# A graph network of four layers on one core: the last node work of two stages moved beside the first units of the next stage, and the tables of the window sums made in two halves

## The chip, the core and the metric

The kernel runs on one core of one Trainium2 chip, as one program. The metric is the device time of one execution in microseconds (us): the median of 3 runs is 2177.65 us, and they lie between 2176.7 and 2178.26. One further execution was profiled; every row below comes from it.

## What is computed

Input are 4096 nodes with 128 features (`x`) and one dense 4096x4096 float32 matrix `adj`, mostly zero. Four layers follow one another, each on a layer norm and ReLU of `x`, each added to `x`:

```
h = relu(layernorm(x)); x = x + L0(h)       # dinv * (adj + I) * dinv @ (h W0^T + b0)
h = relu(layernorm(x)); x = x + L1(h)       # the same with a batch norm of h W1^T + b1 over the nodes
h = relu(layernorm(x)); x = x + L2(h)       # attention:
    xw = h @ W2; el = xw @ a_l; er = xw @ a_r
    attn = where(adj != 0, exp(leaky_relu(el[:, None] + er[None, :])), 0)
    out = (attn / attn.sum(-1)) @ xw + b
h = relu(layernorm(x)); x = x + L3(h)       # three heads and two GRU cells:
    hp = (adj' > 0) @ hW;  hm = (adj' < 0) @ hW          # adj' is adj without its diagonal
    e_plus, e_minus = leaky_relu([hp hm] @ a), leaky_relu([hm hp] @ a)
    att = softmax over the neighbours of e_plus or e_minus, by the sign of adj'
    edge_support = mean over heads of (att * adj') @ hW
    L3 = diag(adj) * gru(adj' @ h, h) + diag(adj) * gru(edge_support, h)
```

## The kernel before, in words

The adjacency matrix doesn't fit on the chip. It is streamed once by rows (to sum the degrees) and then once for each of four passes in **units**: a unit is 128 x 2048 float32 (1 MB), that is, four blocks of 128 source nodes by 512 target nodes. A **chunk** (`c`, 0 to 7) is 512 target nodes and takes 8 units (`g`, 0 to 7), so a pass has 64 units, numbered `n = 8c + g`. The sums of a chunk gather in one or two PSUM banks, and after the chunk its **node work** follows: PSUM to SBUF, turn, scale, add to `x`, norm (statistics on VectorE in `norm_in`, square root on ScalarE in `root`, `norm_out` on VectorE), turn on TensorE (`turn_h`), ReLU on ScalarE, and the next layer's projection (`project` on TensorE, `project_keep` on ScalarE, `agg_project` or `gat_project` on VectorE).

The stages in order of time:

- **deg** sums the rows and makes the first projection.
- **agg0, agg1** are the first two layers. For a unit, ScalarE rounds it to `a_hi` (L502), VectorE takes the rest `a_lo` (L853), and TensorE runs 12 matmuls of 512 columns (L1364 to L1366).
- **gat** is the attention layer. For a unit, VectorE makes half the scores (`gat_max`, L928), ScalarE the other half (L548) and the exponentials (L551, L555), VectorE multiplies with the mask of the unit, in place (L948, the **product**), and TensorE runs 16 matmuls of 129 columns (L1394), each of two passes, so 32 in the profile. The scores of a unit stand in `gunit(n)`, one of three buffers. They need the projection of their targets' chunk (`reg4`) and, for each block of sources, a column of `el02`, `er02`, `er08`, made by ScalarE from `elr` (L518 to L520).
- **edge**, the score pass, sums both score tables `sp_all` and `sm_all` over the positive and the negative neighbours, and `h` over `adj'`. For a unit, VectorE makes two fp8 masks (`masks`, L976 and L977), which are also stored to DRAM, and TensorE runs 8 short matmuls (L1421) and 4 float32 matmuls of 512 columns (L1426, of two passes each, so 8 in the profile). Four pairs of masks fit in `made`.
- **norm**, the sums pass (L1500), reads the stored masks back (`load_masks`, L365) and sums exponentials in windows, so that the softmax can be normalised. Its tables `vp` and `vm` are made by VectorE and ScalarE from the scores of all nodes (L1078 to L1092, "prep"), one after the other: add a shift (3 instructions), cap, exponential on ScalarE (L598, L601), choose, and split into three bf16 parts. The masks come into eight buffers, `kept`. Buffers 4 to 7 lie over the temporaries of the edge GRU cell, so their loads wait for `s_ct["edge"]` to reach 8, the turn of the last chunk's cell (`turn_cells("edge", C)`).
- **out** makes the weights again, multiplies (L1538) and ends with the second GRU cell.

The order of the work is written out by hand: each engine has a program of its own (`@block.tensor` and so on), executes it strictly in that order, and waits on semaphores. `s_ln[p]` counts the norm steps of pass `p`, `s_hturn` the turns of `h`, `s_proj` the projections, `s_pkeep` and `s_pkeep_act` the projections kept, `s_mm[p]` the units multiplied, `s_gy` the products, `s_gexp` the exponentials, `s_mask` the mask pairs, `s_prep` the steps of prep. SyncE issues the unit loads in order into a ring of 8 slots (6 in edge), each when its slot's last unit has been multiplied.

At the end of a stage the node work of its last chunks has nothing beside it. At the handover from agg1 to gat the TensorE program is:

```
                project(p, C - 1)
                turn_sum(p, C)
                turn_h(p, C)
                project(p, C)
            pe.wait_ge(s_pkeep_act, C)
```

and only then come the units of gat. From gat to edge it is `turn_h("gat", C - 1)`, `project`, `turn_h("gat", C)`, `project`, and a wait for all of `s_pkeep["gat"]`. VectorE and ScalarE have the matching ends. From edge to norm TensorE waits for `s_prep` to reach its last step.

Of the kernel before, what the change touches and what calls it, by code (L numbers as in the profile page):

```python
# [39 lines left out]
AHEAD = 2  # L40
GBUFS = 3
# [10 lines left out]
PREP_HEAD, PREP_SIGN = 9, 8  # L52
# [37 lines left out]
def build(nc, x_d, rows_d, cols_d, diag_d, w_d, gru_d, col_d, row_d, masks_d, lines_d, out_d):  # L90
    with ExitStack() as ctx:
# [335 lines left out]
        def _(act):  # L427
# [39 lines left out]

            for p in ("agg0", "agg1"):
# [16 lines left out]
                for c in range(C):  # L485
                    for g in range(G):
# [29 lines left out]
            act.wait_ge(s_pkeep["agg1"], C)  # L516
            elr_v = elr[:, :].rearrange("p (t h) -> p h t", h=2)
            act.activation(el02[:, :], elr_v[:, 0, :], ACT.Exp, scale=SLOPE).then_inc(s_e02, 1)  # L518
            act.activation(er02[:, :], elr_v[:, 1, :], ACT.Copy, scale=SLOPE).then_inc(s_e02, 1)
            act.activation(er08[:, :], elr_v[:, 1, :], ACT.Copy, scale=1 - SLOPE).then_inc(s_e02, 1)  # L520
            act.wait_ge(s_pkeep_act, C)
            act.wait_ge(s_e02, 3)
            act.wait_ge(s_mm["agg1"], G * C)
# [11 lines left out]
            for c in range(C):  # L535
                for g in range(G):
# [149 lines left out]
        def _(dve):  # L686
# [137 lines left out]
            for p in ("agg0", "agg1"):  # L824
# [11 lines left out]
                for c in range(C):  # L836
                    s = Steps(dve, s_ln[p], LN_STEPS[p], c - 1)
                    for g in range(G):
# [17 lines left out]
                agg_project(p, C - 1)  # L856
                s = Steps(dve, s_ln[p], LN_STEPS[p], C - 1)
                agg_nodes_in(p, C, s)
# [741 lines left out]
```

## Time and profile before

| what | us |
|---|---|
| median of 3 runs | 2177.65 |
| profiled execution, its time | 2176.56 |
| profiled execution, span from first to last instruction | 2174.6 |
| TensorE matmuls busy | 1916.5 (88%) |
| VectorE busy | 1650.9 (76%) |
| ScalarE busy | 1245.5 (57%) |
| stage gat, first matmul to last | 653.1 to 928.0 |
| stage edge, first matmul to last unit's end | 945.0 to 1258.5 |
| stage norm, first matmul to last | 1288.2 to 1411.5 |

In the page and the answers, PE is TensorE's matmuls, PEld its weight loads, DVE is VectorE, ACT ScalarE, SP SyncE. A timeline row has start and duration in us, engine, line, operation, output and inputs, shapes, the count of instructions merged, and in brackets the engine's idle time before and what released it. An instruction group's duration runs from its first start to its last end. A row of stretches has the busy time of each engine, then the granted TensorE clock as a share of 2.4 GHz (so 0.50 is 1.2 GHz), the share of DMA and GB/s.

### The profile page before, as it was taken

What the parts mean: (1) busy time and instruction counts of PE and PEld (TensorE: products, weight loads), DVE (VectorE), ACT (ScalarE), POOL (GpSimd) and SP (SyncE); (2) the same over time, 40 slices, a digit from 0 to 9 for tenths busy, and PEclk for the clock granted to TensorE, in tenths of its full rate; (3) what the DMA queues carried; (4) which work ended last, traced back from release to release, by engine and by line L of the source; (5) the groups of instructions that cost most, each with busy time, mean ns of one, the idle gap of its engine ahead of it and who ended that gap; (6) DMA issues with size and microseconds to landing.
All of it is one profiled execution on the core that took longest, in us unless ns stands there. A gap on an engine that the chain in (4) does not pass through costs nothing.

```text
span 2174.6 us, 21337 instructions
## 1 busy us (share of the span) xinstructions
PE 1916.5 (88%) x7805; PEld 1166.7 (54%) x7805; DVE 1650.9 (76%) x2422; ACT 1245.5 (57%) x1386; POOL 0.8 (0%) x7
## 2 busy tenths in 40 slices
PE   2336999699979889879999959999999999999997
PEld 1224888478859888834444426644444444444443
DVE  4668998698849989855655743398898898888985
ACT  3445666366649898800000010198888788887873
POOL 0000000000000000000000000000000000000000
PEclk9999999899989999989999979999999999999998
DMA  9998999488857766659899749732333323233220
GB/s 389 429 429 349 344 338 345 166 306 319 321 194 252 247 222 249 232 181 334 298 321 324 272 162 326 248 99 109 107 122 106 111 102 126 95 118 126 91 83 10
DMA packets 81559, 489.46 MB, mean 225 GB/s; under 512 B 8449, under 2 KB 12546, under 8 KB 36402
## 3 DMA queue, kind: packets, MB, share of 16 engines
q1 hardware_dynamic: 77138, 485.94, 60.9%
q10 hardware_dynamic: 4320, 2.20, 0.3%
q8 instruction: 60, 0.98, 0.2%
q14 instruction: 41, 0.34, 0.1%
HBM read 452.36 MB, written 35.75 MB: 224 GB/s over the span
## 4 chain that ended last, share of the span: by engine, by line
PE 52%; DVE 11%; ACT 6%; issue 1%; DMA 0%; DVEq 0%
PE bank L1538 25%; PE bank L1426 11%; PE bank L1500 5%; PE bank L1394 4%; DVE work L1208 3%; ACT work L555 2%; ACT work L548 2%; PE bank L1421 2%; ACT work L551 1%; DVE reg L1208 1%; PE bank L1449 1%; PE bank L1450 1%; DVE ring L948 1%; PE bank L1520 1%; DVE work L1186 1%
## 5 line engine op out<-in xcount | busy, mean ns | idle before, releaser
L1538 PE MATMUL bank<-work,reg 128*128 128x512 f32 x960 | 423.1, 596 | 17.3 <-DVE ring L1157 11.4
L1208 DVE TENSOR_TENSOR work<-work,ring 128x1536 f32<-128x1536 f32 x160 | 280.5, 1753 | 67.7 <-ACT work L677 66.8
L853 DVE TENSOR_TENSOR a_lo<-ring,a_hi 128x2048 fp32r<-128x2048 f32 x128 | 290.8, 2288 | 31.4 <-ACT a_hi L502 30.5
L1538 PEld LDWEIGHTS bank<-work,reg 128*128 128x128 f32 x960 | 181.9, 191 | 246.7 <-issue 220.3
L502 ACT ACTIVATE a_hi<-ring 128x2048 fp32r<-128x2048 f32 x128 | 244.2, 1913 | 78.5 <-PE bank L1366 78.5
L1394 PE MATMUL bank<-reg,ring 128*128 128x129 f32 x2048 | 243.8, 281 | 34.3 <-DVE ring L948 34.3
L1394 PEld LDWEIGHTS bank<-reg,ring 128*128 128x128 f32 x2048 | 238.2, 197 | 39.2 <-DVE ring L948 29.3
L1538 PE MATMUL bank<-reg 128*128 128x512 f32 x576 | 252.4, 592 | 0.0
L677 ACT ACTIVATE work<-work 128x1536 f32<-128x1536 f32 x160 | 235.3, 1471 | 26.2 <-DVE work L1186 26.2
L1426 PE MATMUL bank<-ring,reg 128*128 128x512 f32 x512 | 237.8, 607 | 0.0
L1364 PE MATMUL bank<-a_hi,s_hi 128*128 128x512 f32 x512 | 207.4, 405 | 20.5 <-DVE a_lo L853 20.5
L1366 PE MATMUL bank<-a_hi,s_lo 128*128 128x512 f32 x512 | 201.9, 394 | 0.0
L1365 PE MATMUL bank<-a_lo,s_hi 128*128 128x512 f32 x512 | 200.7, 392 | 0.0
L1538 PEld LDWEIGHTS bank<-reg 128*128 128x128 f32 x576 | 109.4, 190 | 137.8 <-issue 134.4
L1208 DVE TENSOR_TENSOR reg<-reg,ring 128x1536 f32<-128x1536 f32 x96 | 167.9, 1751 | 0.0
L948 DVE SCALAR_TENSOR_TENSOR ring<-ring,work 128x2048 f32<-128x2048 f32 x64 | 146.6, 2291 | 17.7 <-ACT work L555 17.5
L1426 PEld LDWEIGHTS bank<-ring,reg 128*128 128x128 f32 x512 | 92.4, 190 | 120.0 <-issue 120.0
L653 ACT ACTIVATE work<-reg,ne 128x512 f32<-128x512 f32 x224 | 152.4, 708 | 0.0
L677 ACT ACTIVATE reg<-reg 128x1536 f32<-128x1536 f32 x96 | 141.4, 1472 | 13.6 <-DVE reg L1186 13.6
L1500 PE MATMUL bank<-ring,reg 128*126 128x512 fp8e4 x512 | 115.5, 384 | 20.3 <-DVE reg L1092 16.7
L1364 PEld LDWEIGHTS bank<-a_hi,s_hi 128*128 128x128 f32 x512 | 97.4, 190 | 42.5 <-issue 24.2
L445 ACT ACTIVATE work<-ring 128x2048 f32<-128x2048 f32 x32 | 61.1, 1910 | 101.6 <-DMA ring<-in_adj_rows 101.6
(215 smaller groups left out, 2158.1 us busy)
## 6 DMA issues: line engine op xcount, KB each, us to landing
ring<-in_adj_units SPq DMA_DIRECT2D x320, 1024.0 KB, 4.9
ring<-in_adj_rows SPq DMA_DIRECT2D x32, 2048.0 KB, 17.0
masks<-work SPq DMA_DIRECT2D x64, 512.0 KB, 8.9
ring<-masks SPq DMA_DIRECT2D x64, 512.0 KB, 4.6
reg<-lines SPq DMA_DIRECT2D x8, 768.0 KB, 10.2
ring<-lines SPq DMA_DIRECT2D x8, 768.0 KB, 7.9
out<-ring ACTq DMA_DIRECT2D x8, 256.0 KB, 2.3
gru<-in_cells SPq DMA_DIRECT2D x1, 768.0 KB
```

What stands on the lines that cost most here:

```text
L502: act.activation(a_hi[:, (g % 4) * UNIT:(g % 4 + 1) * UNIT], ring[:, ring_at(p, g)], ACT.Copy).then_inc(s_ahi[p], 1)
L677: act.activation(tiles(n), tiles(n), ACT.Exp, scale=-1.0).then_inc(s_exp, 1)
L853: dve.tensor_tensor(a_lo[:, ring_at(p, g)], ring[:, ring_at(p, g)], a_hi[:, (g % 4) * UNIT:(g % 4 + 1) * UNIT].bitcast(F32), ALU.subtract) ...
L948: dve.scalar_tensor_tensor(y, y, 0.0, gunit(n), ALU.not_equal, ALU.mult).then_inc(s_gy, 1)
L1208: dve.tensor_tensor(tv, tv, spread(ring[:, ring_at("out", g, q * W, W)], HEADS, 1), ALU.mult).then_inc(s_y, 1)
L1364: pe.matmul(acc[:, :], sh, hi, start=begin, stop=False)
L1365: pe.matmul(acc[:, :], sh, lo, start=False, stop=False)
L1366: last = pe.matmul(acc[:, :], sl, hi, start=False, stop=end)
L1394: last = pe.matmul(gat_acc(c, i), y[:, q * W + i * P:q * W + (i + 1) * P], xw[:, m, :], start=m == 0 and i % 2 == 0, stop=m == T - 1 and i ...
L1426: last = pe.matmul(nacc[:, :], reg1[:, t * P:(t + 1) * P], ring[:, ring_at("edge", g, q * W, W, c=c)], start=t == 0, stop=t == T - 1)
L1500: last = pe.matmul(bank[c % 2][0:VCOLS, :], table[:, t * VCOLS:(t + 1) * VCOLS], mask[:, q * W:(q + 1) * W], start=t == 0 and table is vp, ...
L1538: last = pe.matmul(bank[1 + k][:, :], h, tiles(c * T + t)[:, k * W:(k + 1) * W], start=t == 0, stop=t == T - 1)
```

## The change

It does four things.

1. **agg1 to gat.** The tail of agg1's last chunk is taken out of its place and put between gat's first units. On TensorE `turn_h("agg1", C)` comes after gat unit 1 and `project("agg1", C)` after unit 2; a unit of chunk 0 waits for the kept projection of its own sources alone. On VectorE `gat_max(0)` comes first, the node work of the last chunk before unit 0's product, `norm_out` before unit 2's and `agg_project` before unit 4's. On ScalarE the four steps come before units 1 to 4. The columns `el02`, `er02`, `er08` are made in two parts: for source blocks 0 to 23 (`EARLY`) during agg1's last chunk, for 24 to 31 before gat unit 5. Three memsets move behind unit 3's product, one into agg1.
2. **gat to edge.** VectorE makes the masks of units 0 and 1 before the node work of gat's last chunk, those of 2 and 3 inside it, and TensorE runs edge units 0 and 1 before `turn_h("gat", C)`, unit 2 before `project("gat", C)`.
3. **prep in two halves.** `vp` and `vm` are made for source blocks 0 to 15, then for 16 to 31, each with its own exponentials. TensorE waits for the first half before norm unit 0 and for the second before unit 4.
4. ScalarE runs the edge cell's gates after the second exponential of four instead of the first of two.

The diff, cut to its core:

```diff
+EARLY = T - 2 * Q
-PREP_HEAD, PREP_SIGN = 9, 8
+PREP_HEAD, PREP_SIGN, PREP_PARTS = 9, 8, 2
...
+            def exponentials(first, end):
+                act.wait_ge(s_pkeep["agg1"], end // Q)
+                v = elr[:, 2 * first:2 * end].rearrange("p (t h) -> p h t", h=2)
+                tiles_ = slice(first, end)
+                act.activation(el02[:, tiles_], v[:, 0, :], ACT.Exp, scale=SLOPE).then_inc(s_e02, 1)
...
+                        if p == "agg1" and c == C - 1 and g == 6:
+                            exponentials(0, EARLY)
...
                 finish_hT(p, C - 1)
-                project_keep(p, C - 2)
                 keep_sum(p, C)
-                root(p, C - 1)
-                finish_hT(p, C)
-                project_keep(p, C - 1)
                 if p == "agg0":
+                    project_keep(p, C - 2)
+                    root(p, C - 1)
+                    finish_hT(p, C)
+                    project_keep(p, C - 1)
...
-            act.wait_ge(s_pkeep_act, C)
-            act.wait_ge(s_e02, 3)
-            act.wait_ge(s_mm["agg1"], G * C)
+            act.wait_ge(s_pkeep_act, EARLY // Q)
...
+                    if c == 0 and g == 1:
+                        project_keep("agg1", C - 2)
+                    if c == 0 and g == 2:
+                        root("agg1", C - 1)
+                    if c == 0 and g == 3:
+                        finish_hT("agg1", C)
+                    if c == 0 and g == 4:
+                        project_keep("agg1", C - 1)
+                    if c == 0 and g == 5:
+                        exponentials(EARLY, T)
+                    if n < 7:
+                        act.wait_ge(s_e02, 3 if g < EARLY // Q else 6)
                     if n >= GBUFS:
                         act.wait_ge(s_gy, n - GBUFS + 1)
+                    else:
+                        act.wait_ge(s_mm["agg1"], G * C - 3 + n)
...
-            act.wait_ge(s_prep, PREP_HEAD + 2)
-            act.activation(vtmp[1], vtmp[1], ACT.Exp).then_inc(s_vexp, 1)
-            gates("edge", C)
-            act.wait_ge(s_prep, PREP_HEAD + PREP_SIGN + 2)
-            act.activation(vtmp[1], vtmp[1], ACT.Exp).then_inc(s_vexp, 1)
+            for i in range(2 * PREP_PARTS):
+                act.wait_ge(s_prep, PREP_HEAD + i * PREP_SIGN + 2)
+                act.activation(vtmp[1][:, 0:VT // PREP_PARTS], vtmp[1][:, 0:VT // PREP_PARTS],
+                               ACT.Exp).then_inc(s_vexp, 1)
+                if i == 1:
+                    gates("edge", C)
             candidate("edge", C)
...
             gat_max(0)
+            agg_project("agg1", C - 1)
             for c in range(C):
...
+                    if n == 0:
+                        sa = Steps(dve, s_ln["agg1"], LN_STEPS["agg1"], C - 1)
+                        agg_nodes_in("agg1", C, sa)
+                    if n == 2:
+                        dve.wait_ge(s_hturn["agg1"], C - 1)
+                        sa.inc(norm_out(sa, "agg1", C - 1, C))
+                        sa.done()
+                    if n == 4:
+                        agg_project("agg1", C)
+                        clear_tables()
                     if n + 1 < C * G:
                         gat_max(n + 1)
...
-            s = Steps(dve, s_ln["gat"], LN_STEPS["gat"], C - 1)
-            gat_nodes_in(C, s)
-            gat_project(C - 1)
-            gat_nodes_out(C, s)
-            gat_project(C)
...
             masks(0)
+            masks(1)
+            s = Steps(dve, s_ln["gat"], LN_STEPS["gat"], C - 1)
+            gat_nodes_in(C, s)
+            masks(2)
+            gat_project(C - 1)
+            gat_nodes_out(C, s)
+            masks(3)
+            gat_project(C)
...
-            for sign, v in ((0, vp), (1, vm)):
+            for part, sign in itertools.product(range(PREP_PARTS), range(2)):
+                v = (vp, vm)[sign]
+                span = slice(part * T // PREP_PARTS, (part + 1) * T // PREP_PARTS)
...
-            pe.wait_ge(s_pkeep_act, C)
...
+                    if c == 0:
+                        pe.wait_ge(s_pkeep_act, g + 1)
                     pe.wait_ge(s_gy, n + 1)
...
                     last.then_inc(s_gmm, 1)
+                    if n == 1:
+                        turn_h("agg1", C)
+                    if n == 2:
+                        project("agg1", C)
...
             project("gat", C - 1)
-            turn_h("gat", C)
-            project("gat", C)
...
-                        pe.wait_ge(s_ln["gat"], C * LN_STEPS["gat"])
+                        pe.wait_ge(s_ln["gat"], (C - 2) * LN_STEPS["gat"] + GAT_TAKEN)
+                if c == 0:
+                    pe.wait_ge(s_pkeep["gat"], (g + 1) * U_STEPS)
                 pe.wait_ge(s_mask, n + 1)
...
-            pe.wait_ge(s_pkeep["gat"], C * U_STEPS)
             for c in range(C):
                 for g in range(G):
                     edge_unit(c * G + g)
+                    if c == 0 and g == 1:
+                        turn_h("gat", C)
+                    if c == 0 and g == 2:
+                        project("gat", C)
...
-            pe.wait_ge(s_prep, PREP_HEAD + 2 * PREP_SIGN)
...
+                    if c == 0 and g % (G // PREP_PARTS) == 0:
+                        pe.wait_ge(s_prep, PREP_HEAD + (g // (G // PREP_PARTS) + 1) * 2 * PREP_SIGN)
                     pe.wait_ge(s_mload[n % MLOADS], 16 * (n // MLOADS + 1))
```

How the rows stand in the programs (line numbers of the changed file are larger; L1241, L1286, L1288, L1291, L1394 of before are L1288, L1333, L1335, L1338, L1445 there).

**TensorE, end of agg1 and start of gat.** `bank<-ident` is a turn, `hT` and `wts` rows are a projection, `reg,ring` rows gat's units (16 matmuls each). Before, then the change:

```order
L1366 MATMUL bank<-a_hi,s_lo 128x512
L1286 MATMUL bank<-hT,wel 128x512
L1288 MATMUL bank<-wlr,hT 128x2 x4
L1291 MATMUL bank<-wts,hT 128x128 x4
L1241 MATMUL bank<-ident,outT 128x128 x4
L1241 MATMUL bank<-ident,hn 128x128 x4
L1286 MATMUL bank<-hT,wel 128x512
L1288 MATMUL bank<-wlr,hT 128x2 x4
L1291 MATMUL bank<-wts,hT 128x128 x4
L1394 MATMUL bank<-reg,ring 128x129 x288
```

```order
L1413 MATMUL bank<-a_hi,s_lo 128x512
L1333 MATMUL bank<-hT,wel 128x512
L1335 MATMUL bank<-wlr,hT 128x2 x4
L1338 MATMUL bank<-wts,hT 128x128 x4
L1288 MATMUL bank<-ident,outT 128x128 x4
L1445 MATMUL bank<-reg,ring 128x129 x32
L1288 MATMUL bank<-ident,hn 128x128 x4
L1445 MATMUL bank<-reg,ring 128x129 x16
L1333 MATMUL bank<-hT,wel 128x512
L1335 MATMUL bank<-wlr,hT 128x2 x4
L1338 MATMUL bank<-wts,hT 128x128 x4
L1445 MATMUL bank<-reg,ring 128x129 x240
```

The last turn of `hn` now stands behind the first two units of gat, the last projection behind the third; before, both stood ahead of all of them.

**ScalarE, end of agg1 and start of gat.** L474 (L485) is the ReLU into `hT`, L464 and L465 are `project_keep`, L483 is `keep_sum`, L430 (L432) `root`, L518 the first of the columns, L548, L551, L555 (L566, L569, L573) are the scores and exponentials of a unit. Before, all of it stands ahead of unit 0; then, from the changed program, units 1 to 3:

```order
L483 ACTIVATE outT<-bank 128x512
L430 ACTIVATE rstd<-rstd 128x4
L474 ACTIVATE hT<-bank 128x512
L464 ACTIVATE reg<-bank 128x4x128
L465 ACTIVATE reg<-bank 128x512
L518 ACT_TABLE_LOAD
L518 ACTIVATE el<-elr 128x32
L519 ACTIVATE er<-elr 128x32
L520 ACTIVATE er<-elr 128x32
L548 ACTIVATE work<-reg,er 128x512 x2
```

```order
L566 ACTIVATE work<-reg,er 128x512 x2
L569 ACTIVATE work<-work 128x1024
L573 ACTIVATE work<-work,er 128x512 x2
L432 ACT_TABLE_LOAD
L432 ACTIVATE rstd<-rstd 128x4
L566 ACTIVATE work<-reg,er 128x512 x2
L569 ACT_TABLE_LOAD
L569 ACTIVATE work<-work 128x1024
L573 ACTIVATE work<-work,er 128x512 x2
L485 ACTIVATE hT<-bank 128x512
L566 ACTIVATE work<-reg,er 128x512 x2
```

The square root of the last norm now stands between units 1 and 2, with a table load before it and one behind it, and the ReLU before unit 3; before, one load (for L518) followed the square root.

**VectorE, end of gat and start of edge.** L879 to L735 (L900 to L754) are the node work of gat's last chunk, L976 and L977 (L1011, L1012) a pair of masks. Before, then the change:

```order
L948 SCALAR_TENSOR_TENSOR ring<-ring,work 128x2048 x2
L879 TENSOR_TENSOR den<-bank,el 128x2 x2
L882 TENSOR_SCALAR den<-den 128x4
L883 RECIPROCAL den<-den 128x4
L884 TENSOR_TENSOR den<-den,el 128x4
L887 SCALAR_TENSOR_TENSOR x<-bank,den,x 128x128 x4
```

```order
L988 SCALAR_TENSOR_TENSOR ring<-ring,work 128x2048 x2
L995 TENSOR_TENSOR ring<-ring,offdiag 128x128 x4
L1011 TENSOR_SCALAR work<-ring 128x2048
L1012 TENSOR_SCALAR work<-ring 128x2048
L1011 TENSOR_SCALAR work<-ring 128x2048
L1012 TENSOR_SCALAR work<-ring 128x2048
L900 TENSOR_TENSOR den<-bank,el 128x2 x2
L903 TENSOR_SCALAR den<-den 128x4
```

Two pairs of masks now stand between the last product and the node work.

## Rows read from the trace of the kernel before

**Rows 1.** The page, part 1: busy time, share of the span, instructions.

```profile
PE 1916.5 (88%) x7805; PEld 1166.7 (54%) x7805; DVE 1650.9 (76%) x2422; ACT 1245.5 (57%) x1386; POOL 0.8 (0%) x7
```

**Rows 2.** Waits of TensorE: us in total, times, longest us.

```profile
PE bank L1394 <- DVE ring L948: 34.3, 24, 9.6
```

**Rows 3.** Timeline, TensorE at the handover from agg1 to gat.

```profile
625.78 0.40 PE L1366 MATMUL bank<-a_hi,s_lo 128*128 128x512 f32 x1
...
627.68 1.14 PE L1291 MATMUL bank<-wts,hT 128*128 128x128 f32 x8
...
653.06 37.20 PE L1394 MATMUL bank<-reg,ring 128*128 128x129 f32 x310 [9.62 <-DVE ring L948]
```

**Rows 4.** Timeline, ScalarE and VectorE there and in gat's chunk 0.

```profile
629.83 0.60 ACT L483 ACTIVATE outT<-bank 128x512 f32<-128x512 f32 x1
...
631.67 1.13 DVE L811 SCALAR_TENSOR_TENSOR x<-bank,dinv,x 128x128 f32<-128x128 f32 x4 [2.65 <-PE bank L1241]
...
634.26 0.17 DVE L735 TENSOR_SCALAR rstd<-mv 128x4 f32<-128x4 f32 x1
...
652.83 1.00 DVE L928 TENSOR_SCALAR work<-reg,elr,er 128x512 f32<-128x512 f32 x2
...
654.02 2.29 DVE L948 SCALAR_TENSOR_TENSOR ring<-ring,work 128x2048 f32<-128x2048 f32 x1 [0.19 <-ACT work L555]
...
674.40 2.29 DVE L948 SCALAR_TENSOR_TENSOR ring<-ring,work 128x2048 f32<-128x2048 f32 x1 [0.19 <-ACT work L555]
```

**Rows 5.** Timeline, ScalarE at a square root inside gat.

```profile
694.14 1.28 ACT L430 ACT_TABLE_LOAD   x1
```

**Rows 6.** Stretches, TensorE and its granted clock after gat's first matmul.

```profile
656.00:657.00 1.00, 1.00 (x6) 0.50 0.00 0
657.00:658.00 1.00, 1.00 (x7) 0.53 0.00 0
```

**Rows 7.** Timeline, handover from gat to edge.

```profile
920.71 2.29 DVE L948 SCALAR_TENSOR_TENSOR ring<-ring,work 128x2048 f32<-128x2048 f32 x1 [0.16 <-ACT work L555]
...
928.06 0.23 DVE L879 TENSOR_TENSOR den<-bank,el 128x2 f32<-128x2 f32 x2 [5.05 <-PE bank L1394]
...
929.14 1.06 PE L1297 MATMUL bank<-wa,reg 128*128 128x6 f32 x8 [0.69 <-ACT reg L528]
...
934.27 1.11 DVE L742 TENSOR_SCALAR hn<-x,mv,rstd 128x128 f32<-128x128 f32 x4
...
939.87 0.18 DVE L908 COPY work<-bank 128x24 f32<-128x24 f32 x1 [4.49 <-PE bank L1297]
...
941.61 0.89 DVE L960 TENSOR_TENSOR ring<-ring,offdiag 128x128 f32<-128x128 f32 x4
...
944.81 1.22 DVE L976 TENSOR_SCALAR work<-ring 128x2048 fp8e4<-128x2048 f32 x1
...
959.00 0.61 PE L1421 MATMUL bank<-work 128*32 128x512 fp8e4 x8
...
963.18 0.62 PE L1421 MATMUL bank<-work 128*32 128x512 fp8e4 x8
```

**Rows 8.** Timeline, handover from edge to norm.

```profile
1265.31 1.70 DVE L1078 TENSOR_TENSOR work<-e,shift 128x448 f32<-128x448 f32 x3
...
1269.29 1.56 DVE L1086 SCALAR_TENSOR_TENSOR work<-work 128x1344 f32<-128x1344 f32 x1 [1.39 <-ACT work L598]
...
1288.20 0.43 DVE L997 TENSOR_SCALAR ring<-ring 128x512 f32<-128x512 f32 x1
...
1288.22 9.37 PE L1500 MATMUL bank<-ring,reg 128*126 128x512 fp8e4 x32 [16.73 <-DVE reg L1092]
...
1292.34 0.69 DVE L1009 SCALAR_TENSOR_TENSOR ring<-ring 128x512 f32<-128x512 f32 x1
...
1297.42 0.60 PE L1241 MATMUL bank<-ident,ring 128*128 128x128 f32 x4
...
1301.56 8.85 PE L1500 MATMUL bank<-ring,reg 128*126 128x512 fp8e4 x40 [3.54 <-DMA ring<-masks]
```

**Rows 9.** Stretches with all engines, the granted clock between edge and norm.

```profile
1272.00:1280.00 8.00, 0.00 (x0) 0.00 (x0) 7.17 (x8) 1.42 (x3) 0.00 (x0) 0.73 0.45 188
...
1299.00:1301.50 2.50, 0.00 (x0) 0.00 (x0) 0.00 (x0) 0.00 (x0) 0.00 (x0) 1.00 0.98 342
```

More of the change, by code:

```diff
@@ L1 @@
+import itertools
 from contextlib import ExitStack
@@ L837, in _ @@
                     s = Steps(dve, s_ln[p], LN_STEPS[p], c - 1)
+                    if p == "agg1" and c == 1:
+                        dve.memset(xw[:, :, P:P + 1], 1.0)
                     for g in range(G):
@@ L894, in gat_nodes_out @@
             def gat_nodes_out(c, s):
-                dve.wait_ge(s_hkept, c - 1)
+                if c == 1:
+                    dve.wait_ge(s_hturn["agg1"], C)
+                else:
+                    dve.wait_ge(s_hkept, c - 1)
                 s.inc(norm_out(s, "gat", c - 1, c))
@@ L923, in gat_max @@
                 c, g = n // G, n % G
+                if n < 7:
+                    dve.wait_ge(s_e02, 3 if g < EARLY // Q else 6)
+                    dve.wait_ge(s_pkeep_act, EARLY // Q)
                 if n >= GBUFS:
                     dve.wait_ge(s_gy, n - GBUFS + 1)
+                else:
+                    dve.wait_ge(s_mm["agg1"], G * C - 3 + n)
                 for q in (0, 1):
@@ L1072, in _ @@
             s.link(dve.memset(top[:, 16:17], 0.0))
-            for sign, v in ((0, vp), (1, vm)):
+            for part, sign in itertools.product(range(PREP_PARTS), range(2)):
+                v = (vp, vm)[sign]
+                span = slice(part * T // PREP_PARTS, (part + 1) * T // PREP_PARTS)
+                mine = [a[:, 0:VT // PREP_PARTS] for a in vtmp]
+                TP = T // PREP_PARTS
                 e_v = e6[:, :].rearrange("p (t h k) -> p t h k", h=2, k=HEADS)
-                arg, capped, rest = (a.rearrange("p (t v) -> p t v", v=KW) for a in vtmp)
-                parts = [v.rearrange("p (t v) -> p t v", v=VCOLS)[:, :, i * KW:(i + 1) * KW] for i in range(3)]
+                arg, capped, rest = (a.rearrange("p (t v) -> p t v", v=KW) for a in mine)
+                parts = [v.rearrange("p (t v) -> p t v", v=VCOLS)[:, span, i * KW:(i + 1) * KW] for i in range(3)]
                 for k in range(HEADS):
                     last = dve.tensor_tensor(arg[:, :, k * WINDOWS:(k + 1) * WINDOWS],
-                                             e_v[:, :, sign, k:k + 1].to_broadcast([P, T, WINDOWS]),
+                                             e_v[:, span, sign, k:k + 1].to_broadcast([P, TP, WINDOWS]),
                                              shift[:, k * WINDOWS:(k + 1) * WINDOWS].unsqueeze(1)
-                                             .to_broadcast([P, T, WINDOWS]), ALU.add)
+                                             .to_broadcast([P, TP, WINDOWS]), ALU.add)
                 s.link(last)
-                s.inc(dve.tensor_scalar(vtmp[1], vtmp[0], LIFT, None, ALU.min))
-                dve.wait_ge(s_vexp, sign + 1)
-                s.link(dve.scalar_tensor_tensor(vtmp[2], vtmp[0], LIFT, vtmp[1], ALU.is_le, ALU.mult))
+                s.inc(dve.tensor_scalar(mine[1], mine[0], LIFT, None, ALU.min))
+                dve.wait_ge(s_vexp, 2 * part + sign + 1)
+                s.link(dve.scalar_tensor_tensor(mine[2], mine[0], LIFT, mine[1], ALU.is_le, ALU.mult))
                 s.link(dve.tensor_copy(parts[0], rest))
@@ L1384, in _ @@
                     pe.wait_ge(s_ln["gat"], (c - 2) * LN_STEPS["gat"] + GAT_TAKEN)
+                elif c == 1:
+                    pe.wait_ge(s_pkeep_act, C)
+                    pe.wait_ge(s_pkeep["agg1"], C)
                 else:
```

45 lines of the change are left out of this document (22 added, 23 removed).

## The prediction, as it was put on record

> **What bounds the kernel.** I read the page first: TensorE is busy for 88% of the span, VectorE for 76% [rows 1]. So the time is TensorE's, and it can only be won where TensorE stands still or where it follows another engine. The list of waits shows where it follows one: in gat it waits 24 times for VectorE's product, 34.3 us in all, and 9.62 of that is the pause before the first unit [rows 2, 3]. Then I read the timeline at the three handovers that the change touches. From agg1 to gat the last matmul of agg1 ends at 626.2 and gat's first starts at 653.1 [rows 3]; from gat to edge TensorE is free at 930.2 [rows 7] and the first edge matmul comes at 945.0; from edge to norm it waits 16.73 us for the tables and, after four units, 3.54 us more for masks [rows 8]. What an earlier start is worth depends on what paces the stage behind it. In gat's chunk 0 the products come every 3.40 us, (674.40 - 654.02)/6, each 0.19 us after ScalarE's last exponential: ScalarE paces, with VectorE (1.00 + 2.29) close behind [rows 4]. In edge, units stand 4.18 us apart [rows 7], all of it TensorE.
>
> **First handover, agg1 to gat.** I follow the new order with the old durations.
>
> - agg1 ends at 626.2. `keep_sum`, 0.60 [rows 4], no longer waits for the projection of chunk 6 and is done at 626.8. TensorE ends that projection at 628.8 [rows 3] and turns the sum at once, 0.6 as for the turn of the cell [rows 8]: 629.4. The node work, L811 to L735, takes 2.76 [rows 4]: 632.2. Scores 1.0, product 0 2.29: it ends at 635.5. Before, it ended at 652.9 (676.7, the end of product 7 [rows 4], less 7 x 3.40).
> - That is 17.4 us, but ScalarE, the pacing engine, now has the tail's work between its units. Unit 1: the projection kept (2 x 0.60) hides behind VectorE's node work; its exponentials end at 635.6. Unit 2: two table loads of 1.28 [rows 5], 0.2, and 3.5 for the unit: 642.0, product at 644.3.
> - TensorE starts unit 0 at 635.5. A unit is 3.5: ten of them took 37.2 [rows 3], and their first 4.5 us ran at 0.50, 1.2 GHz, until 657.5 [rows 6]. TensorE again comes out of a pause, so unit 0 ends at 641.2 and unit 1 at 644.7. The last turn (0.6) and the ReLU (0.6) follow: ScalarE starts unit 3 at 645.9, and product 3 ends at 651.7. TensorE's unit 2 and the projection (2.8, from 626.0 to 628.8 [rows 3]) end at 651.6, the copies at 652.8, product 4 at 658.6. The second part of the columns adds 0.5: product 5 at 662.5, then 3.4 each, product 7 at 669.3 against 676.7.
> - **7.4 us earlier.** From there VectorE and ScalarE go on as before, so it lasts. Chunk 1's node work needs TensorE's unit 7, done by some 675, and VectorE reaches it at 677.
>
> The row prices a table load at 1.28 us, with the next instruction right behind it. The Trainium skill (ScalarE: Activation LUTs, What ACT_TABLE_LOAD costs) gives about 2.66 us for every switch with the drain, and its rule is to batch by table set, which this edit breaks: by that the two loads would cost 2.8 more, half hidden by TensorE's unit 1, and the gain here would be 5.6. I go by the row. The first part of the columns, with its load, lies in agg1 ahead of ScalarE's last two roundings. TensorE is the engine that ends agg1, so I cost it at nothing; if ScalarE has no lead there, it is 1.28 + 0.6, about 2 us. The memsets (under 1 us) lie in VectorE's wait for ScalarE.
>
> The ends: 0, if TensorE stays at the lower level through units 0 and 1 and the projection (3.5 + 1.3 and 2.8 later); 8.4, if it never falls. I take 7.4, by the clock's return [rows 6].
>
> **Second handover, gat to edge.** The last product ends at 923.0 [rows 7]. Clearing and the first mask pair take 3.2 (941.61 to 944.81), a pair 2.3: 928.5 for two. The node work, the small tables of chunk 6 and the norm took 928.06 to 935.38, 7.3; with pair 2 among them they end at 938.1, pair 3 at 940.4. TensorE is free at 930.2 and runs units 0 and 1 to 938.6 (the clock is up, it has just left gat). `hn` copied (0.6) and turned (0.6): 939.3. Unit 2 to 943.5, projection 1.06 to 944.5, unit 3 to 948.7. VectorE makes the last small tables from 944.5 (939.87 to 941.61, 1.7) and pair 4 by 948.6. With some 0.05 us for each handing over, unit 4 starts at 949.1 against 963.18 [rows 7]: **14 us**, and TensorE paces edge to its end, so all of it lasts. Six units are loaded ahead, and the queue of SyncE has the same order as before, a load behind each store. Ends: 11.7, if one mask pair comes late on this tight path; 14.6, if nothing hands over.
>
> **Third handover, edge to norm.** Now a sign's table takes half of (1288.20 - 1265.31), 11.44 us [rows 8]. An instruction on 1344 elements takes 1.56 and one on 512 0.69: a fixed part of 0.155. Each sign has 11 instructions in its chain (ten of VectorE, one of ScalarE), so half a table takes 5.72 + 11 x 0.155/2 = 6.6. TensorE may start after two, at 1278.5 instead of 1288.2, and runs four units (9.37) to 1287.9. This is 9.7 us earlier, and I expect none of it to last. Unit 4 needs a mask whose buffer is freed by the turn of the edge cell, and the cell stands on VectorE behind all four half tables: 1265.31 + 26.4 = 1291.7, then 4.83 (1288.20 to 1293.03), 1296.5. Before, VectorE had the cell at 1293.0 and TensorE turned it at 1297.4, after its four units. So what was hidden, 4.4 us of slack, is eaten by 3.5 us of added fixed cost: the turn starts 0.9 earlier, takes 0.6 more if the clock is down, the mask load takes its 3.5 as before, and unit 4 starts 0.3 earlier. But TensorE has stood still for 8.6 us before the turn. In the stretch 1272 to 1280, without a matmul, the clock fell [rows 9]; before unit 4, in a pause of 3.5 us behind busy units, it was 1.00 [rows 9]. So unit 4 starts at 1.2 GHz, and some 4.5 us there cost half, 2.3. **Net 2.0 us lost.** Ends: 5 lost, if the 22 added instructions cost twice the fixed part (3.4 later); 4.4 gained, if they are free and the clock stays.
>
> **Sum.** 7.4 + 14.0 - 2.0 = 19.4. The profiled execution takes 2176.6, so 2157.2; the median of the runs shown lies 1.1 above it, at 2177.65, which would give 2158.3. I say 2158. The ends of all three together would be 2170 and 2149.
>
> **The rivals.**
>
> - *The third handover gains.* If the half tables cost no fixed part and the clock holds, the sum is up to 26.8: 2151 to 2155. For it: the 4.4 us of slack. Against it: instructions of 24 elements still take 0.18 [rows 7].
> - *The tail costs ScalarE what it costs.* ScalarE has no spare time in chunk 0. If the loads cost more than the rows say, or the projection runs at 1.2 GHz (2.8 more), the first term is 1 to 3: about 2164. For it: the 0.50 behind a pause [rows 6]. Against it: TensorE works without a pause from 645 to 651.
> - *The second handover doesn't do what it says.* Edge reads 1 MB and writes 0.5 MB in 4.18 us, 376 GB/s, more than the 342 seen beside an idle TensorE [rows 9]. If transfers pace edge once the six loaded units are used, an earlier start is given back there: 2157 + 14, about 2172. Against it: the same pace stood before in the same chunk.
> - *Slower.* TensorE's clock stays at 1.2 GHz through both first chunks, because the tail's pauses are now spread among the first units. Gat units take 7.0: chunk 0 would end at 698 instead of letting node work start at 684.5, 13.8 lost. Eight edge units cost 4.2 more each, 33.4 against 14 won. With the third term, 35 lost: 2212. It decides at 636 to 641: if TensorE isn't at full clock by its unit 2, it is this. Against it: the clock rose 4.5 us after the first unit's start [rows 6].
>
> **How the numbers follow.** Forecast (2154 to 2162) 0.62, third handover gains 0.10, costly tail 0.16, transfers 0.08, slower 0.04. The range of 2152 to 2167 takes in the first, the third and most of the second. About 0.2%, 4.4 us, is what a measurement of this kernel can tell from no change; 2172 is just past it. So faster 0.93, within it 0.03, slower 0.04.
>
> **What would show it.** In the changed profile: product 0 of gat ends near 635.5 and product 7 near 669; TensorE's edge unit 4 starts 21 us earlier than before (7.4 and 14); norm's first matmul comes 31 us earlier, but its unit 4 only some 22; the granted clock is 0.50 at that unit. It is wrong if edge shows waits for masks, if gat's later chunks are longer than before, or if unit 4 of norm moved with unit 0.

## The result, and the profile after

The change takes 2153.26 us (median of 5 runs, 2152.86 to 2155.35) against 2178.26 for the kernel before (5 runs, 2176.7 to 2179.56): a ratio of 0.9888, interval 0.9877 to 0.9899, so 22 to 27 us less. Run again on another occasion (`change_again` below) it gave 0.9894 (0.9878 to 0.9909). The forecast was 2158, within 2152 to 2167. The profiled execution of the change took 2154.86, its span is 2153.1, 21.5 less than before.

The waits of TensorE in the changed kernel (us in total, times, longest):

```profile
PE bank L1445 <- DVE ring L988: 36.8, 26, 6.1
...
PE bank L1288 <- DVE ring L1044: 14.8, 2, 8.6
...
PE bank L1561 <- issue: 8.3, 1, 8.3
...
PE bank L1561 <- DMA ring<-masks: 3.6, 1, 3.6
```

The waits for gat's products are about as long in all as before (36.8 us against 34.3 [rows 2]), in more and shorter pieces. The pause before the first norm unit has gone from 16.73 us [rows 8] to 8.3 (the profile names no releaser for it; it ends 0.1 us behind the second half table), but a new one stands behind it: the turn of the edge cell (L1288) waits 8.6 for the cell (L1044). Then the mask load is waited for as before.

The handover from agg1 to gat, timeline of the changed kernel, TensorE, then VectorE, then ScalarE:

```profile
634.75 9.82 PE L1445 MATMUL bank<-reg,ring 128*128 128x129 f32 x64 [6.09 <-DVE ring L988]
644.41 0.60 PE L1288 MATMUL bank<-ident,hn 128*128 128x128 f32 x4
```

```profile
649.13 2.29 DVE L988 SCALAR_TENSOR_TENSOR ring<-ring,work 128x2048 f32<-128x2048 f32 x1 [4.76 <-ACT work L573]
...
666.33 2.29 DVE L988 SCALAR_TENSOR_TENSOR ring<-ring,work 128x2048 f32<-128x2048 f32 x1 [0.20 <-ACT work L573]
```

```profile
634.74 1.28 ACT L432 ACT_TABLE_LOAD   x1
...
637.48 1.28 ACT L569 ACT_TABLE_LOAD   x1
...
645.04 0.60 ACT L485 ACTIVATE hT<-bank 128x512 f32<-128x512 f32 x1 [3.98 <-PE bank L1288]
```

Unit 0 starts at 634.75 instead of 653.06 [rows 3], but units 0 and 1 take 9.82 us together: the granted clock is 0.50 until 639.8 and 1.00 from there on. ScalarE stands still for 3.98 us until the turn behind them is done, and product 3 waits 4.76 for ScalarE. Product 7 ends at 668.6 instead of 676.7 [rows 4].

The handover from gat to edge, timeline of TensorE:

```profile
921.04 1.06 PE L1344 MATMUL bank<-wa,reg 128*128 128x6 f32 x8 [0.69 <-ACT reg L532]
922.03 0.61 PE L1478 MATMUL bank<-work 128*32 128x512 fp8e4 x8
...
930.69 0.63 PE L1288 MATMUL bank<-ident,reg 128*128 128x128 f32 x4 [0.24 <-ACT reg L537]
...
940.56 0.61 PE L1478 MATMUL bank<-work 128*32 128x512 fp8e4 x8
```

The first edge unit follows the projection of chunk 6 at once, and from there to unit 4 the rows show one wait, 0.24 us. Unit 4 starts at 940.56 against 963.18 [rows 7].

The handover from edge to norm, timeline of VectorE, then TensorE:

```profile
1242.49 1.00 DVE L1125 TENSOR_TENSOR work<-e,shift 128x224 f32<-128x224 f32 x3
...
1269.22 0.43 DVE L1032 TENSOR_SCALAR ring<-ring 128x512 f32<-128x512 f32 x1
```

```profile
1255.92 9.62 PE L1561 MATMUL bank<-ring,reg 128*126 128x512 fp8e4 x32 [8.32 <-issue]
...
1274.12 1.12 PE L1288 MATMUL bank<-ident,ring 128*128 128x128 f32 x4 [8.58 <-DVE ring L1044]
...
1278.81 10.15 PE L1561 MATMUL bank<-ring,reg 128*126 128x512 fp8e4 x40 [3.58 <-DMA ring<-masks]
...
1288.80 0.60 PE L1288 MATMUL bank<-ident,outT 126*128 126x126 f32 x4
```

In the kernel before, that last turn, the first turn of norm's sums, stands here:

```profile
1310.24 0.60 PE L1241 MATMUL bank<-ident,outT 126*128 126x126 f32 x4
```

Norm's first matmul is 32.3 us earlier than before, its unit 4 only 22.75, and the turn behind the five units that start there 21.4: five units that took 8.85 [rows 8] take 10.15. Where the difference of 21.4 us comes from, handover by handover: agg1 itself ended 0.6 earlier in this execution, 7.5 came at the first handover, 14.5 at the second, 0.2 between edge's end and the tables, and 1.4 was lost at the third. The 0.6 is within the spread between executions: agg1 ends between 625.48 and 626.73 in the three profiles whose agg1 is that of the kernel before (`before`, `second_only`, `halves_only`), and between 624.64 and 626.02 in the eleven that have the first part of the columns and a memset in its last chunk.

### The profile page after: what moved, and what is told of

It is laid out like the page before. It is cut to its first block, busy times and chain, and to the rows that moved or that the text cites. A ratio compares the mean times of both kernels' runs of the same rounds, so it can differ in the third digit from the quotient of the medians.

```text
span 2153.1 us, 21391 instructions
## 1 busy us (share of the span) xinstructions
PE 1910.1 (89%) x7805; PEld 1162.6 (54%) x7805; DVE 1652.7 (77%) x2442; ACT 1248.5 (58%) x1393; POOL 0.8 (0%) x7
## 4 chain that ended last, share of the span: by engine, by line
PE 70%; DVE 15%; DMA 7%; ACT 6%; issue 2%; SPq 0%; DVEq 0%; ACTq 0%
PE bank L1599 25%; PE bank L1483 10%; DMA ring<-in_adj_rows 6%; PE bank L1411 5%; PE bank L1413 5%; PE bank L1412 5%; PE bank L1561 5%; PE bank L1445 4%; DVE work L1255 3%; ACT work L573 2%; ACT work L566 2%; DVE a_lo L874 2%; PE bank L1478 2%; DVE reg L1255 1%; PE bank L1288 1%
## 5 line engine op out<-in xcount | busy, mean ns | idle before, releaser
L1599 PE MATMUL bank<-work,reg 128*128 128x512 f32 x960 | 423.0, 596 | 17.3 <-DVE ring L1204 11.4
L1445 PE MATMUL bank<-reg,ring 128*128 128x129 f32 x2048 | 244.9, 281 | 36.9 <-DVE ring L988 36.8
L1445 PEld LDWEIGHTS bank<-reg,ring 128*128 128x128 f32 x2048 | 238.7, 197 | 42.4 <-DVE ring L988 32.5
L696 ACT ACTIVATE work<-work 128x1536 f32<-128x1536 f32 x160 | 235.3, 1471 | 26.1 <-DVE work L1233 26.1
```

Source lines behind the costliest of these rows:

```text
L696: act.activation(tiles(n), tiles(n), ACT.Exp, scale=-1.0).then_inc(s_exp, 1)
L1445: last = pe.matmul(gat_acc(c, i), y[:, q * W + i * P:q * W + (i + 1) * P], xw[:, m, :], start=m == 0 and i % 2 == 0, stop=m == T - 1 and i ...
L1599: last = pe.matmul(bank[1 + k][:, :], h, tiles(c * T + t)[:, k * W:(k + 1) * W], start=t == 0, stop=t == T - 1)
```

## The experiments

Each was run beside the kernel before on one chip, but not all on the same one; the medians of two variants are comparable only through their ratios to the kernel before. Since the medians spread by one or two us, I also measured four stretches in each profile: from agg1's last matmul to the end of gat's product 7, from the end of product 63 to the start of edge unit 4, from the first instruction of the tables to the first turn of norm's sums, and from there to the end. Norm's units 4 to 8, part of the third stretch, have a column of their own.

| kernel | median us (before, same chip) | ratio, interval | agg1 to product 7 | product 63 to edge unit 4 | tables to first turn | of it units 4 to 8 | rest |
|---|---|---|---|---|---|---|---|
| before | - | - | 50.5 | 40.2 | 44.9 | 8.85 | 864.3 |
| the change | 2153.26 (2178.26) | 0.9888, 0.9877 to 0.9899 | 43.0 | 25.7 | 46.3 | 10.15 | 864.3 |
| first_only | 2168.93 (2178.03) | 0.9955, 0.9939 to 0.9972 | 43.5 | 40.5 | 45.1 | 8.85 | 864.4 |
| second_only | 2162.68 (2178.03) | 0.9934, 0.9917 to 0.9951 | 50.1 | 25.7 | 45.1 | 8.85 | 864.4 |
| halves_only | 2178.54 (2178.03) | 1.0003, 0.9993 to 1.0013 | 50.1 | 40.5 | 47.6 | 11.27 | 861.8 |
| no_halves | 2155.35 (2178.03) | 0.9892, 0.9875 to 0.9908 | 43.4 | 25.7 | 45.9 | 10.53 | 864.6 |
| cell_between | 2151.38 (2177.52) | 0.9880, 0.9864 to 0.9897 | 42.8 | 25.7 | 42.0 | 10.66 | 864.5 |
| filler_norm | 2150.32 (2177.52) | 0.9876, 0.9860 to 0.9893 | 42.8 | 25.7 | 44.5 | 8.82 | 861.8 |
| turn_early | 2150.74 (2177.52) | 0.9879, 0.9862 to 0.9895 | 39.1 | 25.7 | 47.9 | 11.69 | 861.8 |
| filler_gat | 2155.29 (2177.52) | 0.9897, 0.9880 to 0.9913 | 41.9 | 25.7 | 47.2 | 11.02 | 864.7 |
| change_again | 2155.17 (2177.69) | 0.9894, 0.9878 to 0.9909 | 43.4 | 25.7 | 48.3 | 11.83 | 861.8 |
| both_mended | 2148.03 (2177.69) | 0.9861, 0.9846 to 0.9876 | 39.1 | 25.7 | 42.0 | 10.69 | 864.6 |
| both_and_filler | 2143.37 (2177.69) | 0.9841, 0.9827 to 0.9854 | 39.8 | 25.7 | 40.2 | 8.85 | 864.2 |
| quarters | 2161.14 (2177.69) | 0.9921, 0.9906 to 0.9936 | 43.1 | 25.7 | 55.3 | 11.40 | 861.8 |

**One part at a time.** `first_only`, `second_only` and `halves_only` hold one handover each; `no_halves` is the change with

```diff
-PREP_HEAD, PREP_SIGN, PREP_PARTS = 9, 8, 2
+PREP_HEAD, PREP_SIGN, PREP_PARTS = 9, 8, 1
```

and the edge cell's gates back behind the first exponential.

> Only the handover from agg1 to gat is changed; the other two stand as in the kernel before. My account (7.4 us won there) expects gat's product 7 to end near 668.6 to 669.3 and the whole to be 7 to 8 us faster than the kernel before, about 2169 to 2170.5. If the tail costs ScalarE what it costs (the costly-tail rival), it is 1 to 3 us. If the measured 25 us of the change contain a gain that is in none of the three handovers, it will show here as more than 9.

> Only the handover from gat to edge is changed. My account expects 14 to 14.5 us less than the kernel before, about 2163 to 2164, with edge unit 4 at some 948.6 instead of 963.2 and every later stage moved by the same. If transfers pace edge, the last edge unit ends less than 5 us earlier and the gain is under 5.

> Only the tables of the sums pass are made in two halves. My account expects a loss of 1 to 2 us against the kernel before (2179 to 2180): norm's first matmul 9 to 10 us earlier, its unit 4 within 0.5 us of before, then the lower clock. The rival (halves gain what TensorE starts earlier) expects 4 to 9 us less, about 2169 to 2174.

> The change with the tables whole again, both other handovers as in the change. My account expects it 1 to 2 us faster than the change, so 23 to 25 us faster than before on the same chip. If the halves won something, it is slower than the change by that much.

The first part alone is worth 9.1 us by the medians (the interval allows 6 to 13) and 7.0 by its stretch. 9.1 is just past the 9 that was to show a gain outside the three handovers, but the profile has none: its other stretches are within 0.4 us of those before, and its span is 6.6 shorter. The second is worth 15.4 by the medians and 14.5 by its stretch. So the costly tail (1 to 3 us) and the transfers as a pace (under 5) are out: in `second_only` edge unit 4 starts 15.7 earlier, of which 1.2 lie ahead of that handover, and the last edge unit is 15.7 earlier too. The halves alone made no difference in the whole (0.5 us more, which the interval doesn't tell from nothing) where 1 to 2 more were expected, but the timeline of TensorE in `halves_only` shows the step:

```profile
1279.59 9.13 PE L1507 MATMUL bank<-ring,reg 128*126 128x512 fp8e4 x32 [7.10 <-issue]
1297.78 1.12 PE L1247 MATMUL bank<-ident,ring 128*128 128x128 f32 x4 [9.07 <-DVE ring L1011]
1302.63 11.27 PE L1507 MATMUL bank<-ring,reg 128*126 128x512 fp8e4 x40 [3.73 <-DMA ring<-masks]
```

The four units start 8.6 us earlier than in the profile of before (9.5 measured from the tables' start, which came 0.8 later in this execution), and unit 4 1.1 later (0.2 from the tables' start), at the lower clock; the stretch is 2.7 longer. That `no_halves` is faster than the change is not shown by the times: it is 22.7 us below the kernel before, where 23 to 25 were expected, the change 25.0 and `change_again` 22.5. By the stretches, four profiles with whole tables (before, `first_only`, `second_only`, `no_halves`) have 44.9 to 45.9 and five with halves and nothing else there (the change, `halves_only`, `turn_early`, `filler_gat`, `change_again`) 46.3 to 48.3: means 45.3 and 47.5. Where it is lost can be read from the rows. Unit 4 starts 35.5 to 36.5 us behind the tables' start in the four and 36.3 to 36.6 in the five, so at that point the halves win and lose almost nothing; the units 4 to 8 behind it take 8.85 in three of the four and 10.53 in `no_halves`, against 10.15 to 11.83 in the five. So the lower clock behind a pause isn't the halves' alone: `no_halves` had it too, with the clock at 0.71 in the first us of unit 4.

Whether this loss lasts to the end of the kernel is not shown. The last stretch of the table is 2.5 us shorter in three of the five (the last section says where), and from the tables' start to the end the four take 909.2 to 910.5 and the five 909.3 to 911.9, which overlap; the means differ by 0.6.

**Who holds norm's unit 4?** `cell_between` moves the cell on VectorE between the halves, and its turn from behind unit 3 to behind unit 1:

```diff
                 s.link(dve.tensor_copy(parts[2], rest))
+                if part == 0 and sign == 1:
+                    sc = Steps(dve, s_gv["edge"], CELL_STEPS, C - 1)
+                    cell_in("edge", C, sc)
+                    cell_end("edge", C, sc)
...
-                    if c == 0 and g == 3:
+                    if c == 0 and g == 1:
                         turn_cells("edge", C)
```

> The change, but VectorE does the last edge cell after the first half of the tables instead of after the second, ScalarE its tanh there, and TensorE turns it after norm unit 1 instead of unit 3, so the masks of units 4 to 7 are fetched early. If the cell's turn and the mask load were what held unit 4, unit 4 now starts when the second half is ready: 1255.9 + 4.9 + 13.4 = 1274.2 instead of 1278.8, 4 to 5 us less than the change, and no wait for masks there. If the cell wasn't the holder, nothing changes.

TensorE in `cell_between`:

```profile
1255.04 5.96 PE L1562 MATMUL bank<-ring,reg 128*126 128x512 fp8e4 x16 [8.51 <-issue]
1260.83 0.60 PE L1289 MATMUL bank<-ident,ring 128*128 128x128 f32 x4
1261.27 3.62 PE L1562 MATMUL bank<-ring,reg 128*126 128x512 fp8e4 x16
1273.09 10.66 PE L1562 MATMUL bank<-ring,reg 128*126 128x512 fp8e4 x40 [8.21 <-DVE reg L1139]
```

The tables began at 1241.60 there and at 1242.49 in the change, so unit 4 starts 31.5 us behind them instead of 36.3: 4.8 earlier, and it waits for the table's last part (L1139), not for masks. The cell and the mask load behind it were the holder. The stretch is 42.0, below the 44.9 to 45.9 of whole tables: with the cell between them, the halves do gain. By the medians it is 26.1 us below the kernel before, 1 to 4 more than the change, with intervals that overlap. Moving the cell with whole tables was not tried.

**Is the fixed part of an instruction what the halves cost?** `quarters` sets `PREP_PARTS` to 4.

> The change with the tables made in four parts instead of two. If a fixed part of 0.155 us an instruction is what makes the halves dear, a part of one sign takes 9.7/4 + 11 x 0.155 + 0.2 = 4.3 us, eight of them 34.7 instead of 26.7, and the turn of the cell and unit 4 come 8 us later: 8 us slower than the change, although TensorE starts norm 4 to 5 us earlier. If the fixed part is an artefact, the tables take 26 to 27 and the time is that of the change or less.

```profile
1251.06 5.15 PE L1561 MATMUL bank<-ring,reg 128*126 128x512 fp8e4 x16 [3.56 <-issue]
1259.61 5.35 PE L1561 MATMUL bank<-ring,reg 128*126 128x512 fp8e4 x16 [3.40 <-DVE reg L1139]
1281.68 1.12 PE L1288 MATMUL bank<-ident,ring 128*128 128x128 f32 x4 [16.72 <-DVE ring L1044]
```

A part of one sign took 4.30 us, all eight 34.4, from 1242.38 to 1276.79 (26.7 in the change, 1242.49 to 1269.22; 22.9 before [rows 8]). Measured from the tables' start, TensorE starts 4.8 earlier and gets the cell 7.7 later, 39.3 us instead of 31.6. The instruction on 1344 elements [rows 8] takes 1.56 us, on 672 in the change 0.86 and on 336 here 0.51, which leaves a fixed part of 0.16 each time. The expected 8 us is 6 (against `change_again`, on the same chip) to 8 by the medians and 7 to 9 by the stretch.

**Does the clock cost what unit 4's neighbours lost?** `filler_norm` keeps TensorE busy with matmuls that nobody reads, in the pause before the cell's turn and behind it:

```diff
                     if c == 0 and g == 3:
+                        pe.wait_ge(s_ga["edge"], 2 * C - 1)
+                        for _ in range(8):
+                            pe.matmul(bank[6][:, :], reg1[:, 0:P], reg2[:, 0:W], start=True, stop=True)
                         turn_cells("edge", C)
+                        for _ in range(3):
+                            pe.matmul(bank[6][:, :], reg1[:, 0:P], reg2[:, 0:W], start=True, stop=True)
```

> The change, plus eight matmuls of 512 columns whose result nobody reads between norm unit 3 and the turn of the cell, and three between the turn and unit 4. If it is the clock that costs some 1.3 us after unit 4, the granted clock is 1.00 at unit 4 (0.50 in the change), units 4 to 8 take 8.9 instead of 10.2 us, and it is 1.3 us faster in the stretches. If the filler runs too long, the turn comes later by that.

Stretches in the change, then in `filler_norm` (TensorE, PEld, VectorE, ScalarE and POOL busy, then the granted clock, DMA share, GB/s):

```profile
1266.00:1274.00 8.00, 0.00 (x0) 0.00 (x0) 6.99 (x11) 0.63 (x1) 0.00 (x0) 0.62 0.00 0
...
1277.00:1280.00 3.00, 1.19 (x3) 0.75 (x4) 0.00 (x0) 0.00 (x0) 0.00 (x0) 0.50 1.03 407
1280.00:1284.00 4.00, 4.00 (x16) 2.39 (x15) 0.00 (x0) 0.00 (x0) 0.00 (x0) 0.81 1.01 410
```

```profile
1266.00:1274.00 8.00, 6.13 (x18) 2.78 (x17) 6.25 (x10) 0.63 (x1) 0.00 (x0) 1.00 0.00 0
...
1277.00:1280.00 3.00, 2.46 (x12) 1.62 (x13) 0.00 (x0) 0.00 (x0) 0.00 (x0) 1.00 1.02 391
```

and its timeline of TensorE from unit 4 on:

```profile
1277.54 8.82 PE L1561 MATMUL bank<-ring,reg 128*126 128x512 fp8e4 x40 [1.03 <-DMA ring<-masks]
```

The clock fell to 0.50 (1.2 GHz) in the pause of the change and stayed at 1.00 beside the filler. Five units take 8.82 instead of 10.15, and the turn of the cell 0.66 instead of 1.12. The stretch is 44.5, 1.8 below that of the change and 2.9 below the mean of the five, and 1.3 of the 1.8 are in units 4 to 8 and 0.5 at the turn: it was the clock. By the medians it is 27.2 us below the kernel before, 2 to 5 more than the change.

**What holds gat's product 3?** `turn_early` moves two calls on TensorE by one unit:

```diff
-                    if n == 1:
+                    if n == 0:
                         turn_h("agg1", C)
-                    if n == 2:
+                    if n == 1:
                         project("agg1", C)
```

> The change, but TensorE turns the last h of agg1 after gat unit 0 instead of 1 and projects it after unit 1 instead of 2. ScalarE's wait of 3.98 us before the ReLU of product 3 should go to under 1, product 3 end near 648, product 7 near 665.3 instead of 668.6: 3 to 3.6 us faster. If ScalarE's own work is the bound there (costly tail), under 1.

`filler_gat` leaves the order and puts six such matmuls in TensorE's pause before gat unit 0:

```diff
+                else:
+                    for _ in range(6):
+                        pe.matmul(bank[7][:, :], wel[:, :], hT[:, :], start=True, stop=True)
```

> The change, plus six matmuls of 512 columns whose result nobody reads in TensorE's pause of 6.09 us before gat unit 0. If the lower clock in units 0 and 1 costs what I took for it, those two take 7.4 instead of 9.8 us, the turn comes 2.3 earlier and product 7 ends 1 to 2 us earlier. If not, nothing.

TensorE, then ScalarE, in `turn_early`:

```profile
639.81 0.60 PE L1288 MATMUL bank<-ident,hn 128*128 128x128 f32 x4
```

```profile
640.45 0.60 ACT L485 ACTIVATE hT<-bank 128x512 f32<-128x512 f32 x1
...
646.66 0.60 ACT L466 ACTIVATE reg<-bank 128x512 f32<-128x512 f32 x1 [2.23 <-PE bank L1338]
```

TensorE in `filler_gat`:

```profile
628.94 5.32 PE L1428 MATMUL bank<-hT,wel 128*128 128x512 f32 x12
635.19 7.38 PE L1448 MATMUL bank<-reg,ring 128*128 128x129 f32 x64 [0.94 <-DVE ring L988]
642.41 0.60 PE L1288 MATMUL bank<-ident,hn 128*128 128x128 f32 x4
```

The wait of 3.98 us is gone in `turn_early`, and product 7 ends 39.1 us behind agg1 instead of 43.0, 3.9 earlier. In `filler_gat` the two units take 7.38 instead of 9.82, ScalarE waits 1.55, and product 7 comes 1.2 earlier. So it was the place of the turn in TensorE's order, not ScalarE's own work, that held units 3 and 4, and the clock was less than a third of it. In `turn_early` ScalarE still waits 2.23 us for the projection. By the medians `turn_early` is 26.8 us below the kernel before, 2 to 4 more than the change; `filler_gat` is 22.2 below, and its whole time shows nothing of the 1.2 us.

**Together.** `both_mended` joins `turn_early` and `cell_between`; `both_and_filler` adds eight filler matmuls behind norm unit 3. `change_again` is the change.

> The change itself, unaltered, beside the kernel before on the same chip. The three stretches of its profile add up to some 21 us less, while the medians so far say 25. If the medians are right and the profiled execution of before was a quick one, 24 to 25 us again; if they were chance, 21 to 22.

> The change with both mends: the last turn of agg1 one unit earlier, and the edge cell between the halves of the tables. The two act in different stages, so 3.9 and 5.3 us should add: 9 us less than the change, about 2145 to 2146.

> As both_mended, plus eight matmuls of 512 columns whose result nobody reads in TensorE's pause of some 8 us before norm unit 4. If the clock is what costs there, the granted clock at unit 4 is 1.00, units 4 to 8 take 8.9 instead of 10.7 us, and it is 1.5 to 2 us less than both_mended. If not, the same.

`change_again` gave 22.5 us less than before by the medians, so of the 25 first measured some 3 are spread; the spans of the two profiled executions are equal, 2153.1. `both_mended` is 7.1 faster than it by the medians, where 9 were expected, and 8.7 faster by its span (2144.4 against 2153.1). `both_and_filler` is the fastest, 34 us less than the kernel before. Its unit 4 and the four behind it:

```profile
1271.04 8.85 PE L1562 MATMUL bank<-ring,reg 128*126 128x512 fp8e4 x40 [0.91 <-DVE reg L1139]
```

The granted clock is 1.00 there, the five units take 8.85 us instead of 10.69, as forecast, and the stretch 40.2 instead of 42.0. Its median is 4.7 below that of `both_mended`, with intervals that overlap; the stretch explains 1.8 of it, and the spans of the two profiled executions differ by 0.5 only.

## Why the prediction came out as it did

- **First handover, 7.4 forecast, 7.5 measured.** Every step of the chain is there: products 0 and 7 were to end at 635.5 and 669.3 and ended at 634.6 and 668.6 with agg1 0.6 earlier; unit 0 at the lower clock; ScalarE's wait for the turn. One row was misread on the way: in [rows 6] the mean of 0.53 between 657 and 658 has the clock rise at 657.9, not 657.5, and units 0 and 1 took 9.82 us where 9.2 were worked out; with `filler_gat`'s 7.38 the lower clock cost 2.4. The two table loads took 1.28 us each, as in [rows 5]. Each started at most 0.02 us behind the end of the instruction before it (634.72 and 634.74 at the first), and ScalarE's next instruction 0.02 us behind the load; the gain is the one worked out from that row. The Trainium skill (ScalarE: Activation LUTs, What ACT_TABLE_LOAD costs) gives about 2.66 us for a switch, of which about 1.38 are a drain, by which the handover was to gain 5.6, an estimate from that page; the trace shows no such drain and disagrees.
- **Second handover, 14 forecast, 14.5 measured.** It was sized with allowances for handing over that were hardly needed: without them the sum was 948.7, and less the 8.1 us from ahead that is 940.6, where unit 4 started. The tight place, mask pair 4, was as tight as worked out: VectorE ended it at 940.42, and unit 4 started at 940.56, less than 0.2 us later than behind unit 3 without a wait.
- **Third handover, 2.0 lost forecast, 1.4 lost measured in the change**, 2.2 on the mean of five profiles against four. The mechanism held: half a table 6.68 us where 6.6 were worked out, the turn 23.3 us earlier than before (of which 22.6 are from ahead, agg1's 0.6 and the two handovers), the clock at 0.50. The forecast gain of 0.9 at the turn was 0.5 (23.3 less the 22.6 and the 0.2 that came between edge's end and the tables), and unit 4 started, from the tables' start, 0.1 later where 0.3 earlier were forecast. The clock's part was put at 0.6 on the turn and 2.3 behind unit 4; it was 0.5 on the turn, and behind unit 4 1.3 in the change and 2.2 to 3.0 in the other four profiles. What the prediction didn't have is that this part differs from one execution to the next. Against the kernel before, the whole time shows no such loss beyond its spread (`halves_only` 0.5 us slower, interval 1.5 faster to 2.8 slower).
- **The sum** was 19.4 and the spans differ by 21.5. Of the 2.1 between them 0.6 is agg1, 0.1 the first handover, 0.5 the second, 0.2 lies between edge's end and the tables, and 0.6 is the third. The median moved by 25.0 at first and 22.5 on repetition. The working gave 2158.3 (named as 2158), and 2153.26 is 5.0 below. 2.3 of them are the terms above (2157.2 worked out for a profiled execution, 2154.86 measured); 2.7 come from placing the median on one profiled execution, which I took to lie 1.1 below the median and which lay 1.6 above it. By the number alone the result lies outside the main case (2154 to 2162) and in the band of the rival in which the third handover gains (2151 to 2155), though that handover gained nothing; that it is still inside the range of 2152 to 2167 is partly luck. What speaks for the account are the rows of each handover, not the total.
- **The rivals.** Costly tail and transfers are excluded by `first_only` and `second_only`; beside that, the transfers ran at 407 to 410 GB/s in the change's norm stretches above, so the 342 that the rival went by was no limit. Slower is excluded by the granted clock, which is 1.00 from 639.8 on, before unit 1 begins (the sign was to be read at 636 to 641). That the third handover gains is true only once the cell is moved out of the way (`cell_between`): the cell behind all four half tables is what the prediction named as the reason for no gain.

## What to carry to other kernels

When work is split so that a consumer can start earlier, look for the consumer's second wait: here the first four units started 9.5 us sooner behind the tables' start, and the fifth no sooner, since it hung on another step, queued behind all the parts on the same engine. Put that step between the parts. When tail work goes between the first units of the next stage, place each piece of the chain at the earliest unit at which its input is ready: one unit too late cost 3.9 us of a possible 11.4 (7.5 and 3.9).

## What the runs showed of the hardware

The last stretch of the table, from norm's first turn to the end, has two values, 861.8 in five profiles and 864.2 to 864.7 in nine, in kernels with the same code there. In the change and in `change_again` TensorE's rows at the very end differ:

```profile
2131.16 4.54 PE L1581 MATMUL bank<-ring,wts 128*128 128x512 f32 x6 [1.98 <-DVE ring L1204]
```

```profile
2132.86 2.84 PE L1581 MATMUL bank<-ring,wts 128*128 128x512 f32 x6 [1.98 <-DVE ring L1204]
```

After the same pause of 1.98 us the same six matmuls took 4.54 us in one execution and 2.84 in the other; the granted clock over the 5 us from 2131 on was 0.66 in the first, and 1.00 in the 5 us from 2133 on in the second. Some 0.8 us more lies in the first matmuls of the out pass, behind a pause of 5.84 us in both. The two places go together: in the five profiles with 861.8 the six matmuls take 2.84 us, and from the start of the out pass to the turn behind its first 24 matmuls it is 11.8 to 12.1; in the nine others 4.54 and 12.8 to 13.4. All five are kernels with split tables; whether that has a part in it wasn't tried, but the change and `change_again` are one program and fell on either side. So whether this pause of 1.98 us costs the clock was not settled by its length in these runs: it differed between executions of one program, and a difference of 2.5 us between two profiles may be this alone. The third handover's loss of 1.4 to 3.3 us in the five profiles is of the same kind: unit 4 starts within 0.3 us in all five, and the rest of the spread is in units 4 to 8, 10.15 to 11.83 us. What decides it wasn't tried.
